# A decoder layer's prologue on one core: batch 0 first, first distances in half blocks, next projections behind them

## What is computed

```python
P = layernorm(x) @ W_in + b_in          # per head: Q, K, V, G of 64 each
Q, K, V, G = split(P, 4)
d2 = q2[..., :, None] + k2[..., None, :] - 2.0 * (Q @ K.T)
W = (EPS + sqrt(max(d2, 0))) ** -2
W = W / (EPS + sum(W, -1))
x = x + concat(G * (W @ V)) @ W_out + b_out
x = x + cross_attention(layernorm(x), ctx, mask)   # keys, values from ctx
x = x + experts(layernorm(x))
```

## Time and profile before

| | |
|---|---|
| median of 3 runs | 1659.29 us (1654.48 to 1662.12) |
| the profiled execution | 1656.51 us, span 1654.3 us |
| mean granted TensorE clock | 0.936 |
| busy: PE, DVE, ACT, POOL | 88%, 63%, 56%, 39% |
| DMA | 66.9 MB, 40 GB/s on the mean |

### The profile page before, as it was taken

One profiled execution on the slowest core, in us unless ns is written; L12 is line 12 of the kernel. 1 busy time (PEld: TensorE's weight loads), 2 busy tenths in 40 slices (PEclk: granted clock), 3 DMA queues, 4 the chain that ended last, 5 costly groups with the idle time before them and its releaser, 6 DMA issues. The chain is left out here.

```text
span 1654.3 us, 23058 instructions
## 1 busy us (share of the span) xinstructions
PE 1453.9 (88%) x7425; PEld 934.3 (56%) x7426; DVE 1039.0 (63%) x1352; ACT 926.9 (56%) x643; POOL 643.0 (39%) x476
## 2 busy tenths in 40 slices
PE   4659999999999999999998759988996499999996
PEld 3434555455554555555554347777775366666664
DVE  6457889889988889889888555455555521222121
ACT  1049888998889888998889812222222022222221
POOL 1304546554465546554455432212211133333331
PEclk9769999999999999999999779889886699999998
DMA  4000000000000000000000042111120033333312
GB/s 125 19 7 1 14 26 25 13 13 25 25 19 13 19 25 25 13 13 25 19 13 13 5 142 91 38 46 49 38 90 19 13 79 92 75 84 84 81 29 70
DMA packets 67467, 66.90 MB, mean 40 GB/s; under 512 B 5136, under 2 KB 59920, under 8 KB 67408
## 3 DMA queue, kind: packets, MB, share of 16 engines
q1 hardware_dynamic: 60144, 56.58, 10.5%
q0 software_dynamic: 7296, 9.97, 3.6%
HBM read 48.70 MB, written 19.92 MB: 41 GB/s over the span
## 5 line engine op out<-in xcount | busy, mean ns | idle before, releaser
L927 DVE TENSOR_SCALAR wts<-ps_s,k 128x1024 f32<-128x1024 f32 x256 | 316.9, 1280 | 108.4 <-PE ps_s L510 89.3
L1519 POOL TENSOR_TENSOR v_aug<-v_aug,wts 128x1024 f32<-128x1024 f32 x96 | 255.9, 2666 | 295.6 <-ACT wts L1372 291.1
L1364 ACT ACTIVATE wts<-wts 128x4096 f32<-128x4096 f32 (+1 forms) x80 | 232.0, 2936 | 140.9 <-DVE wts L927 140.7
L522 PE MATMUL ps_o<-wts,g_r 128*64 128x512 f32 x1024 | 253.8, 618 | 12.2 <-ACT wts L1372 12.0
L1370 ACT ACTIVATE wts<-wts,eps_d 128x4096 f32<-128x4096 f32 (+1 forms) x80 | 241.7, 3021 | 0.2
L1372 ACT ACTIVATE wts<-wts 128x4096 f32<-128x4096 f32 (+1 forms) x80 | 235.3, 2941 | 2.5
L736 PE MATMUL ps_s<-wts,qk 128*128 x608 | 198.0, 469 | 3.1 <-issue 2.3
L1300 DVE TENSOR_TENSOR wts<-rinv,ps_s 128x352 f32<-128x352 f32 x76 | 39.6, 521 | 253.9 <-ACT rinv L1437 170.9
L510 PE MATMUL ps_s<-q_hi,k_hi 64*128 64x512 f32 x512 | 117.2, 452 | 58.2 <-DVE wts L927 49.7
L916 DVE TENSOR_TENSOR v_aug<-v_aug,wts 128x1024 f32<-128x1024 f32 x96 | 158.7, 1653 | 10.0 <-ACT wts L1372 9.7
L736 PEld LDWEIGHTS ps_s<-wts,qk 128*128 128x128 f32 x608 | 110.5, 191 | 64.8 <-issue 17.0
(11 more groups left out here) (219 smaller groups left out, 2413.2 us busy)
## 6 DMA issues: line engine op xcount, KB each, us to landing
wts<-in_w SPq DMA_DIRECT2D x16, 704.0 KB
h_t<-o_raw SPq DMA_DIRECT2D x16, 512.0 KB, 2.6
qk<-h_t SPq DMA_DIRECT2D x16, 512.0 KB, 4.1
wts<-in_w SPq DMA_DIRECT2D x8, 640.0 KB
wts<-in_x SPq DMA_DIRECT2D x2, 2048.0 KB, 8.7
raw_qk<-in_w_in SPq DMA_DIRECT2D x32, 128.0 KB, 2.2
raw_vg<-in_w_in SPq DMA_DIRECT2D x32, 128.0 KB, 2.2
acc<-wts SPq DMA_DIRECT2D x17, 128.0 KB, 1.7
```

The costliest lines, as they stand in the source:

```text
L522: mm = pe.matmul(ps_o[r, t], v_pair[:, b, r], wts[:, h, b, t], start=b == 0, stop=b == SB - 1)
L927: dve.tensor_scalar(wts[:, h, b, :], ps_s[:, h, :], k2[:, 2 * b + h:2 * b + h + 1], 0.0, ALU.add, ALU.max).then_inc(S_.max_ok, 1)
L1364: act.activation(chunk(start, end), chunk(start, end), ACT.Sqrt).then_inc(S_.sqrt_ok, 1)
L1519: pool.tensor_tensor(acc_w[:, 0], acc_w[:, 0], wts[:, 0, b], ALU.add).then_inc(S_.add_ok, 1)
```

## The change

SP loads x of batch 0 alone, then constants, q and k weights of pair 0 and the biases, then x of batch 1; a new semaphore `cst_in` counts constants and biases alone, and the context's loads move behind the weights of pair 1. VectorE normalises batch 0; TensorE turns its 16 pieces, projects q and k of pair 0 into different banks (`project_first`), takes v next and the key norms in `ps_o`. ScalarE loads its root table at the start and makes `q_hi` and `k_hi` of pair 0. VectorE takes batch 1's statistics between those steps, GpSimd normalises batch 1, and its pieces are turned behind blocks 3 and 4 of the distances. The distances of pair 0 go in half blocks of 512 columns (`distances` with `fill`, `guard_halves`), each half with its own count. q and k of pair 1 and g of pair 0 are projected behind the last block. The context is prepared at the start of the last pair. The line numbers of the changed kernel differ from those of before.

```diff
-        x_first = wts[:, 1, 0:4, :].rearrange("p a (b d) -> p (a b) d", d=D)
+        x_first = [wts[:, 1, a:a + 2, :].rearrange("p a (b d) -> p (a b) d", d=D) for a in (0, 6)]
         zeros = wts[:, 1, 4, 0:D]
...
-        C_IN = 16 * (1 + 8 + DC + 4 + 1 + 4 + 1 + 1)
-        xn = wts[:, 0, 0:4, :].rearrange("p a (b d) -> p (a b) d", d=D)
+        C_IN, CST_IN = 16 * (DC + 4 + 1 + 4 + 1 + 1), 16 * (1 + 8)
+        xn = [wts[:, 0, a:a + 2, :].rearrange("p a (b d) -> p (a b) d", d=D) for a in (0, 6)]
...
-            sp.dma_start(cst[:], consts).then_inc(S_.c_in, 16)
+            sp.dma_start(x_first[0], x[0].rearrange("(n p) d -> p n d", p=P)).then_inc(S_.x_in, 16)
+            sp.dma_start(cst[:], consts).then_inc(S_.cst_in, 16)
...
+            load_qk(0, 0)
...
+                    sp.dma_start(b_all[h * DH:(h + 1) * DH, k], src).then_inc(S_.cst_in, 16)
+            sp.dma_start(x_first[1], x[1].rearrange("(n p) d -> p n d", p=P)).then_inc(S_.xb_in, 16)
+            load_vg(0, 0)
+            sp.wait_ge(S_.zero_ok, 1)
+            sp.dma_start(y_rows[NT * P:], zeros).then_inc(S_.zero_out, 16)
+            sp.dma_start(acc[NT * P:], zeros).then_inc(S_.zero_out, 16)
+            load_qk(1, 1)
...
+            def turn_rows(k):
+                n, c = k // DC, k % DC
+                if n < 2:
+                    pe.wait_ge(S_.xn_ok, n + 1)
+                    dst = ps_s[:, k // 2, (k % 2) * HALF:(k % 2 + 1) * HALF]
+                else:
+                    pe.wait_ge(S_.xnb_ok, 1)
+                    pe.wait_ge(S_.v_ok, 1)
+                    if k >= 6:
+                        pe.wait_ge(S_.xnt_ok, k - 1)
+                    dst = ps_o[:, (k % 2) * HALF:(k % 2 + 1) * HALF]
+                for i in range(4):
+                    mm = pe.transpose(dst[:, i * P:(i + 1) * P], xn[n // 2][:, 4 * (n % 2) + i, c * P:(c + 1) * P], ident)
+                mm.then_inc(S_.tr_ok, 1)
...
+            def context():
+                pe.wait_ge(S_.c_in, C_IN)
+                pe.wait_ge(S_.max_ok, NB * PAIRS)
...
+            def project_first():
+                pe.wait_ge(S_.wqk_ok, 2)
+                for k, out in enumerate((ps_p, ps_s[:, 1])):
+                    for i in range(STEPS):
+                        if k == 0 and i % (STEPS // 2) == 0:
+                            pe.wait_ge(S_.xnt_ok, 2 + 2 * (i // (STEPS // 2)))
+                        mm = project_step(out, wqk_hi, wqk_lo, 0, k, i)
+                    mm.then_inc((S_.q_proj, S_.k_proj)[k], 1)
...
-            def norm_k(n):
+            def norm_k(n, out):
                 pe.wait_ge(S_.sqk_ok, n + 1)
-                pe.wait_ge(S_.qn_ok, n + 1)
+                if not (isinstance(n, int) and n == 0):
+                    pe.wait_ge(S_.qn_ok, n + 1)
...
             def project_v(n, keys):
                 pe.wait_ge(S_.wvg_ok, 2 * n + 2)
-                pe.wait_ge(S_.k_cp, keys)
+                if keys is not None:
+                    pe.wait_ge(S_.k_cp, keys)
+                else:
+                    pe.wait_ge(S_.q_ok, 1)
...
             def turn_v(n):
                 pe.wait_ge(S_.vt_ok, n + 1)
-                pe.wait_ge(S_.kv_ok, 1)
-                if not (isinstance(n, int) and n == 0):
+                if isinstance(n, int) and n == 0:
+                    pe.wait_ge(S_.k2_ok, 1)
+                else:
                     pe.wait_ge(S_.oraw_ok, n)
...
+                fill = isinstance(n, int) and n == 0
...
-                    done = 1 if isinstance(n, int) and n == 0 else n
-                    pe.wait_ge(S_.vt_ok, done)
-                    pe.wait_ge(S_.g_ok, done)
-                else:
+                    if not fill:
+                        pe.wait_ge(S_.vt_ok, n)
+                        pe.wait_ge(S_.g_ok, n)
+                elif not fill:
                     pe.wait_ge(S_.max_ok, NB * n + 2 * b)
                 s_blk = slice(b * P, (b + 1) * P)
                 for th in range(2):
+                    if fill and b:
+                        pe.wait_ge((S_.fill_ok, S_.max_ok)[th], (b, 2 * b)[th])
...
-                mm.then_inc(S_.s_ready, 1)
+                    if fill:
+                        mm.then_inc(S_.fill_s, 1)
+                if not fill:
+                    mm.then_inc(S_.s_ready, 1)
...
+                if ahead == 0:
+                    context()
...
-            project_qk(0, 0, 2 * STEPS, None)
+                    norm_k(p + 2, ps_s[:, 0])
+            pe.wait_ge(S_.cst_in, CST_IN)
+            for k in range(4):
+                turn_rows(k)
+            project_first()
             norm_q(0)
-            norm_k(0)
-            pe.wait_ge(S_.k_cp, 1)
-            project_qk(1, 0, 2 * STEPS, None)
-            project_g(0)
-            project_v(0, 2)
-            turn_v(0)
+            project_v(0, None)
+            norm_k(0, ps_o)
             for b in range(SB):
                 distances(0, b)
+                if b == 0:
+                    turn_v(0)
+                if b == 3:
+                    turn_rows(4)
+                    turn_rows(5)
+                if b == 4:
+                    turn_rows(6)
+                    turn_rows(7)
+            project_qk(1, 0, 2 * STEPS, None)
+            project_g(0, ps_p, 2)
             norm_q(1)
-            norm_k(1)
+            norm_k(1, ps_s[:, 0])
...
+            def guard_halves(b):
+                for th in range(2):
+                    t = slice(th * HALF, (th + 1) * HALF)
+                    dve.wait_ge(S_.fill_s, 2 * b + th + 1)
+                    for h in range(2):
+                        g = dve.tensor_scalar(wts[:, h, b, t], ps_s[:, h, t], k2[:, 2 * b + h:2 * b + h + 1], 0.0, ALU.add, ALU.max)
+                        if th:
+                            g.then_inc(S_.max_ok, 1)
+                        elif h:
+                            g.then_inc(S_.fill_ok, 1)
...
+            def turned_low(k):
...
+                dve.wait_ge(S_.xh_ok, k + 1)
+                dve.tensor_tensor(xn_lo[:, c, n * HALF:(n + 1) * HALF], src, xn_hi[:, c, n * HALF:(n + 1) * HALF].bitcast(F32),
+                                  ALU.subtract).then_inc(S_.xnt_ok, 1)
+            row_stats(0)
+            row_aggr(0)
+            row_rstd(0)
             dve.wait_ge(S_.rstd_ok, 1)
-            for i in range(NT):
...
-            context()
+            row_stats(1)
             copy_q(0)
+            row_aggr(1)
             copy_k(0)
-            split_high(0)
+            row_rstd(1)
             split_low(0)
             norm_rows(0)
             copy_k2(0)
+            copy_vt(0, 1)
+            for b in range(SB):
+                if b == 4:
+                    dve.wait_ge(S_.zero_out, 32)
+                guard_halves(b)
+                if b == 0:
+                    copy_v(0)
+                if b == 3:
+                    turned_low(4)
+                    turned_low(5)
+                if b == 4:
+                    turned_low(6)
+                    turned_low(7)
             copy_q(1)
             copy_k(1)
+            split_high(1)
+            norm_rows(1)
             copy_g(0)
-            copy_vt(0, 1)
-            copy_v(0)
-            dve.wait_ge(S_.zero_out, 32)
-            dve.wait_ge(S_.k2_ok, 1)
-            for b in range(SB):
-                guard(0, b, None)
-            split_high(1)
             split_low(1)
-            norm_rows(1)
             copy_k2(1)
...
+            act.preload_act_table_set("sqrt_and_others")
+            row_std(0)
+            for k in range(4):
+                turned_high(k)
+            act.wait_ge(S_.q_ok, 1)
+            act.activation(q_hi[:], q32[:], ACT.Copy)
+            row_std(1)
+            act.wait_ge(S_.k_cp, 1)
+            act.activation(k_hi[:], k32[:], ACT.Copy).then_inc(S_.hi_ok, 1)
...
+                    if isinstance(n, int) and start in (2, 4):
+                        turned_high(start + 2)
+                        turned_high(start + 3)
...
-            pool.wait_ge(S_.c_in, C_IN)
+            pool.wait_ge(S_.cst_in, CST_IN)
             split_qk(0)
             split_vg(0)
             square_q(0, None)
             square_k(0)
             split_qk(1)
+            pool.wait_ge(S_.rstd_ok, 2)
+            for i in range(SB):
+                bn = pool.tensor_scalar(xn[1][:, i, :], x_first[1][:, i, :], mean_var[:, SB + i, 0:1], rstd[:, SB + i:SB + i + 1],
+                                        ALU.subtract, ALU.mult)
+            bn.then_inc(S_.xnb_ok, 1)
             square_q(1, 1)
...
+            pool.wait_ge(S_.c_in, C_IN)
```

170 lines of the change are left out of this document (84 added, 86 removed).

## The result

The changed kernel takes **1604.9 us** (median of 4 runs, 1602.33 to 1609.18) against 1660.07 us beside it: 0.9674 of the time, 95% interval 0.965 to 0.9697, 55 us less. The profiled execution took 1605.31 us, its span is 1603.5 us. The forecast was 1613, in a range of 1601 to 1627: the direction and the range held, the gain was 11 us larger.

The account below looks back on a forecast made before the run. TensorE bounds the loop from 129 us on, so prologue time won counts fully. First value matmul at 85 instead of 129.1 gives 44, plus 0.5 (pair 0), minus 0.5 (context): 1613, between 1612.5 and 1615.3; range 1601 to 1627.

Parts of the forecast that it names:

- main case: Whole prologue: first value matmul at 85 instead of 129.1, gain 38 to 50 us; chance 0.62.
- last at 58 to 69, first value matmul at 79 to 92: Signs that would show the forecast right: end of pair 0's last distance matmul and start of its first value matmul, in us.
- Stage A: Start to first distance matmul: 32 us instead of 73.3, ends 30 and 36.
- Stage B: Distances of pair 0, in half blocks: 31 us instead of 43.6, ends 26 and 36.
- I take 3.1, the middle, as in the rows about half the blocks ran at each pace: Distances of pair 0: time per block, between 2.65 us fast and 3.5 slow; 24.8 us for eight blocks.
- the cover of GpSimd's normalisation: Batch 1's normalisation done by 33 to 40 us, TensorE asking at about 45: cover at least 5 us, cost nothing.
- Stage C: Last distance matmul to first value matmul, one dependent chain: 21.9 us instead of 12.2, ends 18 and 25.
- The pairs and the context: Later pairs stay at 52.6 us each, 0.5 won in pair 0; context in the last pair loses 0.5 us.
- Everything at the fast pace: Rival for the prologue: three stages of 30, 26 and 18 us, 55 us won, 1601 to 1604; chance 0.13.
- Low clock: Rival: TensorE at its lower level through the prologue, first value at 97, 32 us won, 1624 to 1627; chance 0.18.
- Halves do not overlap: Rival in pair 0's distances: blocks stay near 5 us, 43 us in all, 32 us won, 1624 to 1627; chance 0.05.
- Slower: Rival: GpSimd's eight normalisations delay TensorE, gain gone from 7.3 us each, 1666 at 8.5 us each; chance 0.02.

Follow-up runs that it names:

- kernel 8: Changed kernel with the cross-attention context (loads, matmuls, VectorE part) ahead of q0 again; median 1620.1 us, first value matmul at 90.1.
- kernel 4: Changed kernel with q1, k1 and g0 projected and copied ahead of the first distances again; median 1612.3 us, first value matmul at 81.5.
- kernel 2: Kernel before the change with half blocks in the distances of pair 0 and nothing else changed; median 1637.8 us, first value matmul at 106.2.
- kernel 3: Kernel before the change, whole blocks kept, ten unread matmuls put behind each block but the last to fill TensorE's waits; median 1653.7 us.
- kernel 1: Changed kernel with whole blocks in the distances of pair 0 again, two guards of 1024 columns each; median 1623.6 us, first value matmul at 87.6.
- kernel 10: Changed kernel with q1 in the distances, k1 in the values' bank, pair 1's high parts on ScalarE, query norms and norm rows earlier; median 1599.5 us.
- the repeat: The changed kernel timed and profiled again, unchanged; median 1604.4 us, first value matmul at 76.3.
- kernel 5: Changed kernel with both batches loaded, normalised on VectorE and transposed ahead of q0; median 1614.0 us, first value matmul at 83.7.
- kernel 9: Changed kernel with q1 projected in two TensorE waits among the distances and k1 in the values' bank; median 1600.0 us, first value matmul at 71.4.
- kernel 11: Kernel 10 with the high parts of q1 and k1 back on VectorE, ahead of the norm rows; median 1599.4 us, first value matmul at 70.0.
- kernel 7: Changed kernel with GpSimd's eight normalisations done twice, first into unread tiles; median 1613.6 us, first value matmul at 83.3.

## Why the prediction was right, and where not

The range and the direction held, and the main case (a gain of 38 to 50 us) did not: its signs "last at 58 to 69, first value matmul at 79 to 92" came at 56.7 and 74.8. The stages and their chains were right, and the sizes in two of them were off.

*Stage A, 32 forecast, 31.4 came.* The half load was usable at 6.5 us (6.2 forecast), statistics took 2.7, normalisations 3.5 for 4.1, transposes started at 12.9 (12.5), the key norms' copy ended at 31.2 for 30.8. The clock was at full there. That context, q1, k1 and g0 left this path is shown by kernels 8 and 4.

*Stage B, 31 forecast, 25.3 came.* This is the step that was mis-sized most, in the term "I take 3.1, the middle, as in the rows about half the blocks ran at each pace". Where nothing stands between, blocks came every 2.7 us, at the fast end of 2.65: 21.6 us for the eight, for 24.8 forecast. The slow pace of the rows was not a state of the chip that the change inherits, but an effect of the waits that the change removes: kernels 2 and 3 show it, the one by overlap, the other by filling. I had costed the overlap at the average of two clocks when it sets the clock itself. The other 2.3 us are in what is put in between, forecast at 4 us for TensorE's transposes and 2 for two stalls, and 3.7 came. It is VectorE's work that shows there, the copy of v (1.22) and four low parts (1.28 and 1.29), since VectorE bounds the fill. The half guard was 0.68 us (0.66 forecast), and the cover of GpSimd's normalisation held. TensorE's two long waits, 1.26 us behind the copy of v and 1.87 behind batch 1's low parts, made 3.1.

*Stage C, 21.9 forecast, 18.1 came.* The same error in four terms. q1 and k1 were taken at 4.0 us, the middle of the two paces, and g0 at 3.5; each took 3.1 on TensorE, with a wait of VectorE of 3.14 for k1, the figure that the fast row of before had shown. The key norms, taken at 3.2 beside a row of 3.54 us from a stretch at a granted clock of 0.64, took 1.9 at 1.00, the largest single part of the miss. The chain itself was right: q1, copy, k1, copy, g0, query norms, rows, key norms. ScalarE did not hold it. Undoing the placement loses 6.7 us (kernel 4).

*The pairs and the context.* From the first distances of pair 1 to the load of the output weights behind the pairs lie 822.4 us, 824.6 before; in the twelve other kernels 822.4 to 824.9. The pairs give nothing back. The context costs 0, for 0.5 forecast: kernel 8, whose last pair has none, took 822.8.

*The rivals.* "Everything at the fast pace" (0.13, first value at 74, 55 us won, 1601 to 1604) is what happened, to 1 us; it should have been the main case. That the time lies in the stated range is owed to the range having taken this rival in. Its counter-argument, that q1 had run slow in the kernel before, was drawn from a projection behind TensorE's longest wait of that stretch, and the granted clock was 0.53 from 50 to 61 us (timeline of before, the matmuls just ahead of q1's):

```profile
52.35 3.55 PE L466 MATMUL ps_s<-cst,k_sq 128*128 128x2 f32 x16 [8.95 <-DVE q_n L876]
```

"Low clock" fell. The Trainium skill (TensorE: Matmul & The Clock Gate, section on psum-queue depth-cycling) spoke for it: a kernel that cycles through banks with short idles swings between the levels. The traces agree where TensorE waits 2.6 us for VectorE (0.70 before, 0.89 in kernel 1). For the halves, which cycle through the same four banks with waits of 0.2 us and, in the change, two of 1.26 and 1.87, they agree only in part: 1.00 in the change and in kernels 2 and 10, but 0.93 to 0.94 in the repeat and in kernels 4, 5, 8, 9 and 11, each with one short stretch at a low clock. "Halves do not overlap" fell by VectorE's idle time of 0.2 us ahead of its 32 half guards. "Slower" did not come near; kernel 7 shows the price.

*The sum.* Undone one at a time, the parts moved the first value matmul by 12.8 (halves), 15.3 (context), 8.9 (batch 0 first) and 6.7 us (projections behind): 43.7 of 54.3, each uncertain by the 1.5 us above. The rest belongs to edits not tried alone (separate banks for k0, v0 moved ahead, high parts on ScalarE) and to the parts working together; it stays open how it divides.

## What to carry to other kernels

When TensorE takes turns with another engine and its granted clock is low there (0.70 here), look for the wait first: splitting the hand-over in halves gave the overlap and the clock together, here 13.5 and 8.5 us of a stretch of 43.6. In a forecast, a duration measured beside a wait must not be used for the version in which that wait is gone; ask which level each row was taken at and why. Work that has slack at the end of a loop (the context in the last pair) cost nothing there and 15 us on the first path.
